# One core: the causal convolution of 64 heads, rewritten from full Toeplitz blocks to chunks of 256 samples with carried modal states

## The reference, cut to what matters

```
# layer 0: per head h a causal convolution along the 1024 samples
dt = exp(log_dt[h]);  A = -exp(log_A_real) + i*A_imag          # 64 modes per head
K[h, l] = 2*Re( sum_n C[h,n]*(exp(dt*A[h,n])-1)/A[h,n] * exp(dt*A[h,n]*l) )
u = x * (sample < length[sequence])
y = causal_conv(u, K[h]) + D[h]*u
x = x + mask * y
# layer 1: per row (1024 samples as features)
base   = x @ W.T ;  logits = x @ Wr.T + 5*onehot(language)     # 8 experts
gates  = softmax over the top 2 logits
x = x + base + 2 * sum_e gates[e] * (x @ A[e].T) @ B[e].T      # rank 16
```

## Time and profile before

| what | value |
|---|---|
| median of the runs | 749.24 us |
| profiled execution: span | 747.6 us |
| profiled execution: own time | only its span is on record; the runs lie 1.6 us above it |
| TensorE busy | 724.0 us (97%), 4453 matmuls |
| weight loads | 707.0 us (95%) |
| VectorE busy | 357.8 us (48%) |
| ScalarE busy | 282.1 us (38%) |
| GpSimd busy | 31.0 us (4%) |
| mean granted TensorE clock | 0.994 of 2.4 GHz |

### The profile page before, as it was taken

One profiled execution on the slowest core, in us unless ns is written; L12 is line 12 of the kernel. 1 busy time (PEld: TensorE's weight loads), 2 busy tenths in 40 slices (PEclk: granted clock), 3 DMA queues, 4 the chain that ended last, 5 costly groups with the idle time before them and its releaser, 6 DMA issues.

```text
span 747.6 us, 11954 instructions
## 1 busy us (share of the span) xinstructions
PE 724.0 (97%) x4453; PEld 707.0 (95%) x4453; DVE 357.8 (48%) x891; ACT 282.1 (38%) x388; POOL 31.0 (4%) x37
## 2 busy tenths in 40 slices
PE   3799999999999999999999999999999999999997
PEld 2689999999999999999999999999999999999997
DVE  8884453543454444455344444455345544334431
ACT  4755333453324433343333442345332433333111
POOL 4030100010000100001000010001000000000000
PEclk9899999999999999999999999999999999999999
DMA  7661523217221263213432152321722125321002
GB/s 241 197 192 29 130 98 113 84 28 226 55 77 67 58 196 112 84 28 97 130 112 84 28 156 83 99 84 28 226 87 60 50 68 187 112 84 29 11 20 56
DMA packets 23545, 72.99 MB, mean 98 GB/s; under 512 B 4522, under 2 KB 5866, under 8 KB 23530
## 3 DMA queue, kind: packets, MB, share of 16 engines
q1 hardware_dynamic: 18250, 56.01, 25.8%
q10 hardware_dynamic: 5280, 16.78, 6.8%
HBM read 55.71 MB, written 17.07 MB: 97 GB/s over the span
## 4 chain that ended last, share of the span: by engine, by line
PE 95%; DVE 3%; issue 1%; ACT 0%; DMA 0%; ACTq 0%; SPq 0%; DVEq 0%
PE pmg L929 55%; PE pc L889 25%; PE pmg L904 6%; PE px L895 4%; PE px L861 4%; PE pmg L850 1%; PE pmg L926 0%; DVE w_lo L648 0%; DVE ex_q L572 0%; DVE toe L627 0%; DMA logs<-in_L_cond_log_A_real 0%; ACT result L464 0%; DVE xt L704 0%; DVE toe L575 0%; DVE toe L620 0%
## 5 line engine op out<-in xcount | busy, mean ns | idle before, releaser
L929 PE MATMUL pmg<-w_hi,y_hi 128*128 128x388 f32 (+1 forms) x768 | 264.5, 344 | 0.0
L929 PE MATMUL pmg<-w_hi,y_lo 128*128 128x388 f32 (+1 forms) x768 | 260.2, 339 | 0.0
L929 PE MATMUL pmg<-w_lo,y_hi 128*128 128x388 f32 (+1 forms) x768 | 259.8, 338 | 0.0
L889 PE MATMUL pc<-u,t_hi 128*128 128x512 f32 (+4 forms) x640 | 167.5, 345 | 1.2 <-DVE t_lo L777 1.2
L929 PEld LDWEIGHTS pmg<-w_hi,y_hi 128*128 128x128 f32 x768 | 144.2, 188 | 2.0
L929 PEld LDWEIGHTS pmg<-w_hi,y_lo 128*128 128x128 f32 x768 | 144.5, 188 | 0.0
L929 PEld LDWEIGHTS pmg<-w_lo,y_hi 128*128 128x128 f32 x768 | 144.2, 188 | 0.0
L889 PE MATMUL pc<-u,t_lo 128*128 128x512 f32 (+7 forms) x512 | 124.2, 304 | 0.0
L889 PEld LDWEIGHTS pc<-u,t_hi 128*128 128x128 f32 x640 | 112.3, 188 | 8.5 <-issue 1.4
L678 DVE TENSOR_TENSOR u<-xt,u 128x1024 fp32r<-128x1024 f32 x30 | 36.8, 1226 | 118.1 <-ACT xt L422 76.6
L889 PEld LDWEIGHTS pc<-u,t_lo 128*128 128x128 f32 x512 | 82.6, 189 | 3.7
(11 more groups left out here) (160 smaller groups left out, 615.3 us busy)
## 6 DMA issues: line engine op xcount, KB each, us to landing
toe<-kpad SPq DMA_DIRECT2D x31, 1024.0 KB, 7.0
rows<-in_x SPq DMA_DIRECT2D x64, 256.0 KB, 7.3
out<-result ACTq DMA_DIRECT2D x62, 256.0 KB, 5.7
result<-in_L_cond_W SPq DMA_DIRECT2D x3, 512.0 KB, 7.7
rows<-in_L_cond_W SPq DMA_DIRECT2D x2, 512.0 KB, 6.8
toe<-in_L_cond_W SPq DMA_DIRECT2D x2, 512.0 KB, 4.6
toe<-in_L_cond_B SPq DMA_DIRECT2D x1, 512.0 KB, 5.2
xt<-in_L_cond_W SPq DMA_DIRECT2D x1, 512.0 KB, 8.5
```

Source lines behind the costliest of these rows:

```text
L889: ins = nc.tensor.matmul(pc[:, h, d:CH, :], t[s][:, h, d * P:(d + 1) * P], v[s][:, 0:n, tok], start=(d == 0 and v is u_hi and t is t_hi), ...
L929: ins = nc.tensor.matmul(pm[:, n, 0:c1 - c0], y[s][:, c, :], w[:, c, c0:c1], start=(c == 0 and y is y_hi and w is w_hi), stop=(c == CH - 1 ...
```

## The change

K is no longer made for 1024 lags but for 256 (SPAN). Inside a chunk of 256 samples the convolution is a Toeplitz product with two block lags (the diagonal one over all 8 blocks, 512 columns, and the next over every second block, 256 columns). What reaches over a chunk's edge goes through 64 complex modes per head, held as 128 real numbers: `control` multiplies the samples of chunks 0 to 2 with the powers of the modes (c_hi, c_lo, the turned table Z), `carry` rotates by a per-head factor and scans the three chunk states, and in `convolve` the states (s_hi, s_lo) are multiplied with the powers zo_hi, zo_lo and added to chunks 1 to 3. All products take three passes.

New for each pair are `turn_powers` (4 transposes of Z into the upper half of px), `split_ctr`, `split_obs`, `copy_states` (4 ScalarE instructions), `carry` (18 VectorE instructions in five stages, each behind a wait on the one before) and `split_states`. Gone are `copy_far`, two additions in `merge`, and three quarters of the Toeplitz tile. K and the powers are made for 4 heads (DUO), once in two pairs, and the table Z is 4 x 256 = 1024 wide; its argument and magnitude are made by 8 ScalarE instructions with per-partition scales instead of two GpSimd products. GpSimd stages per-head scalars. The loop body is two pairs. toe, t_hi, t_lo and the c tiles have one buffer, so the load of the next four heads' Toeplitz tile waits for t_lo of the last pair that used the old one. The start is reordered, with 73 parameter steps.

```diff
-            def convolve(b, m, first=False, turned=True):
...
-                    for d in range(CH):
-                        n = CH - d
-                        near = d < FAR
-                        for t, v in ((t_hi, u_hi), (t_hi, u_lo), (t_lo, u_hi)) if near else ((t_lo, u_hi),):
-                            ins = nc.tensor.matmul(pc[:, h, d:CH, :], t[s][:, h, d * P:(d + 1) * P], v[s][:, 0:n, tok],
-                                                   start=(d == 0 and v is u_hi and t is t_hi), stop=d == CH - 1)
+            def convolve(b, m, first=False):
...
+                for h in range(2):
+                    tok = slice(h * SEQS, (h + 1) * SEQS)
+                    three(pc[:, h, :, :], (t_hi[:, h, 0:P], t_lo[:, h, 0:P]),
+                          (u_hi[s][:, :, tok], u_lo[s][:, :, tok]), True, False)
+                    three(pc[:, h, 1:CH:2, :], (t_hi[:, h, P:SPAN], t_lo[:, h, P:SPAN]),
+                          (u_hi[s][:, 0:CH:2, tok], u_lo[s][:, 0:CH:2, tok]), False, False)
+                pe.wait_ge(zhi_ready, i + 1)
+                pe.wait_ge(zlo_ready, i + 1)
+                pe.wait_ge(shi_ready, i + 1)
+                pe.wait_ge(slo_ready, i + 1)
+                for h in range(2):
+                    for q in range(2):
+                        at = slice(q * P, (q + 1) * P)
+                        ins = three(pc[:, h, 2 + q:CH:2, :], (zo_hi[s][:, h, at], zo_lo[s][:, h, at]),
+                                    (s_hi[:, h, :, :], s_lo[:, h, :, :]), False, q == 1)
+                ins.then_inc(conv_done, 1)
+            def control(b, m):
...
+                for h in range(2):
+                    tok = slice(h * SEQS, (h + 1) * SEQS)
+                    for q in range(2):
+                        ins = three(v_psum[:, h, :, :], (c_hi[:, h, q, :], c_lo[:, h, q, :]),
+                                    (u_hi[s][:, q:CH - 2:2, tok], u_lo[s][:, q:CH - 2:2, tok]), q == 0, q == 1)
 # TensorE, one step
                 if rows_left:
                     turn_rows(b, m + 2)
-                convolve(b, m + 1, turned=rows_left)
-                if kernels and m == 1:
-                    make_kernels(b + 1)
-                project(b, m)
+                convolve(b, m + 1)
+                pe.wait_ge(yhi_ready, 2 * b + m + 1)
+                pe.wait_ge(ylo_ready, 2 * b + m + 1)
+                project_bank(b, m, 0)
+                if rows_left:
+                    control(b, m + 2)
+                if ahead:
+                    turn_powers(b, m + 3)
+                if kernels and m == 1:
+                    make_kernels(b + 2)
+                project_bank(b, m, 1)
+                project_bank(b, m, 2, kernels)
 # ScalarE, one step
+                if kernels and m == 1:
+                    waves(b + 2)
+                if rows_left:
+                    split_toe(b, m + 2)
+                split_y(b, m + 1)
+                if ahead:
+                    split_obs(b, m + 3)
+                ratios(b, m)
+                if rows_left:
+                    copy_states(b, m + 2)
+                if ahead:
+                    split_ctr(b, m + 3)
+                if kernels and m == 0:
+                    act.wait_ge(gen_staged, b + 1)
+                    turns_of(None, True)
+                    magnitudes(None, True)
+                if kernels and m == 1:
+                    copy_kernels(b + 2)
+                split_gated(b, m)
+                if rows_left:
+                    split_states(b, m + 2)
+                finish(b, m)
 # VectorE, one step
                 if rows_left:
                     split_rows(b, m + 2)
                 merge(b, m + 1)
+                if rows_left:
+                    split_toe(b, m + 2)
+                if kernels and m == 1:
+                    powers(b + 2)
+                split_y(b, m + 1)
+                if ahead:
+                    split_obs(b, m + 3)
+                route(b, m)
+                if ahead:
+                    split_ctr(b, m + 3)
+                if rows_left:
+                    dve.wait_ge(scan_staged, b + m // 2 + 1)
+                    carry(b, m + 2)
+                split_gated(b, m)
+                if kernels and m == 0:
+                    angles(b + 2)
+                if rows_left:
+                    split_states(b, m + 2)
+                if kernels and m == 1:
+                    first_samples(b + 2, bass.ds((b + 2) * DUO, DUO))
 # VectorE, carry: 18 instructions, five stages
+                for h in range(2):
+                    add(S[:, h, :, :], swapped[:, h, :, :], k(C2_IM, h), S[:, h, :, :])
+                for h in range(2):
+                    ins = vec.tensor_scalar(R[:, h, :, :], swapped[:, h, two, :], k(C2_RE, h), None, ALU.mult)
+                ins.then_inc(scan, 1)
+                dve.wait_ge(scan, SCAN * i + 1)
+                for h in range(2):
+                    add(R[:, h, :, :], v_psum[:, h, two, :], k(C2_NIM, h), R[:, h, :, :])
+                for h in range(2):
+                    ins = add(S[:, h, 1, :], S[:, h, 0, :], k(A_RE, h), S[:, h, 1, :])
+                ins.then_inc(scan, 1)
...
 # SyncE
+            def load_toe(g, split=None):
+                sp.wait_ge(k_stored, 16 * g + 16)
+                if split is not None:
+                    sp.wait_ge(tlo_ready, split)
...
+                if ahead:
+                    sp.wait_ge(px_full, i + 2)
+                    load_rows(b, m + 3)
+                if kernels and m == 1:
+                    store_kernels(b + 2)
+                    load_toe(b + 2, 2 * b + 4)
```

More of the change, by code:

```diff
@@ L76, in cond_resid_kernel @@
         xt = [sb(f"xt{s}", [P, CH, P]) for s in range(2)]
[L77 to L82, removed]
+        u_hi = [sb(f"u_hi{s}", [P, CH, P], F32R) for s in range(2)]
+        u_lo = [sb(f"u_lo{s}", [P, CH, P], F32R) for s in range(2)]
+        t_hi = sb("t_hi", [P, 2, SPAN], F32R)
+        t_lo = sb("t_lo", [P, 2, SPAN], F32R)
+        c_hi = sb("c_hi", [P, 2, 2, P], F32R)
+        c_lo = sb("c_lo", [P, 2, 2, P], F32R)
+        zo_hi = [sb(f"zo_hi{s}", [P, 2, SPAN], F32R) for s in range(2)]
+        zo_lo = [sb(f"zo_lo{s}", [P, 2, SPAN], F32R) for s in range(2)]
+        state = sb("state", [P, 2, CARRIED, SEQS])
+        swapped = sb("swapped", [P, 2, CARRIED, SEQS])
+        turned_s = sb("turned_s", [P, 2, CARRIED - 1, SEQS])
+        s_hi = sb("s_hi", [P, 2, CARRIED, SEQS], F32R)
+        s_lo = sb("s_lo", [P, 2, CARRIED, SEQS], F32R)
         y_hi = [sb(f"y_hi{s}", [P, CH, P], F32R) for s in range(2)]
@@ L372, in _ @@
[L372 to L386 removed]
+            at = pos_far[:, :].unsqueeze(1).to_broadcast([P, HEADS, FARS])
@@ L522, in _ @@
+                finish(b, m)
+            with act.Fori(0, LOOPS) as b:
+                for m in range(2):
+                    step(b, m)
+            step(LOOPS, 0, kernels=False)
+            step(LOOPS, 1, ahead=False, kernels=False)
+            step(LOOPS + 1, 0, rows_left=False, ahead=False, kernels=False)
+            ratios(LOOPS + 1, 1)
+            split_gated(LOOPS + 1, 1)
+            finish(LOOPS + 1, 1, last=True)
             act.wait_ge(result_dma[0], START + 16 * PAIRS)
@@ L862, in turn_rows, with three @@
                 ins.then_inc(px_full, 1)
-            def convolve(b, m, first=False, turned=True):
-                i, s = BODY * b + m, m % 2
+            def three(out, left, right, first, last):
+                (l_hi, l_lo), (r_hi, r_lo) = left, right
+                for n, (l, r) in enumerate(((l_hi, r_hi), (l_hi, r_lo), (l_lo, r_hi))):
+                    ins = nc.tensor.matmul(out, l, r, start=first and n == 0, stop=last and n == 2,
+                                           skip_group_check=True)
+                return ins
@@ L953, in _ @@
-            convolve(0, 0, first=True)
-            for k in range(LATE, WTILES):
-                turn_weight(k)
-            def step(b, m, rows_left=True, kernels=True):
+            turn_weight(0)
+            turn_weight(1)
+            pe.wait_ge(par_dve, C1_STEPS)
+            turn_parameters(C1_RE)
+            pe.wait_ge(par_dve, C2_STEPS)
+            turn_parameters(C2_RE)
+            pe.wait_ge(uhi_ready, 1)
+            turn_powers(0, 0)
+            turn_weight(2)
+            turn_weight(3)
@@ new lines, in _ @@
+            pe.wait_ge(gk_ready, 1)
+            pe.wait_ge(prm_ready, 4)
+            make_kernels(0, staged=False)
+            control(0, 0)
+            turn_powers(0, 1)
+            for k in range(4, 7):
+                turn_weight(k)
+            turn_rows(0, 1)
+            turn_weight(7)
+            turn_weight(8)
+            convolve(0, 0, first=True)
+            control(0, 1)
+            turn_powers(0, 2)
+            pe.wait_ge(k_copied, 1)
+            make_kernels(1, staged=False)
@@ new lines, in step @@
+                project_bank(b, m, 1)
+                project_bank(b, m, 2, kernels)
+            with pe.Fori(0, LOOPS) as b:
+                for m in range(2):
```

(8 more changed lines are left out.)

890 lines of the change are left out of this document (494 added, 396 removed).

## The result

The changed kernel takes 754.65 us (754.19 to 755.12, four runs) against 749.23 (749.13 to 749.26): ratio 1.0073, interval 1.0059 to 1.0087. It is slower by 0.7% where 2.6% faster was forecast. The span is 753.0 us, forecast 728.4. Ratios compare runs at the usual clock alone: one execution of a later kernel (e6) took 991.73 us at a granted clock of 0.66, where its others had 0.97 to 0.98, nothing here explains it, and it is left out of that kernel's figures.

What follows compares the result with a forecast made beforehand. TensorE was taken as the bound, VectorE's queue to gt_lo stalling each step 0.45 us. Start 71.3, even steps 306.8, odd 294.0, then 19.6, 17.7 and 19.0: span 728.4, forecast 730 us against 749.24, range 710 to 756.

Steps and rivals of the forecast that it cites:

- loop starts: Start of the loop: forecast at 67.3 us against 45.39 before, plus 2 us low clock at the first convolution.
- steps 29, 30 and the rest: End of the kernel: 19.6 us without kernels and powers, 17.7 without rows and control, last projection to span end 19.0.
- The step that failed: VectorE's queue in a step: u_lo starts 4.19 us in, or 4.63 where the loop's edge falls, in each even step.
- The table load's price: ScalarE: a table load takes 1.28 us with no drain behind it; the skill page says 2.66 in all.
- The queue's other terms: VectorE and ScalarE ahead of gt_lo: carry 4.6 us (ends 3.3 and 5.8), four state copies 1.6, overlay 1.35.
- slower queue: Rival: VectorE's queue sets the step, with carry at 5.8 us between c_lo and gt_lo; 767 us, chance 15%.
- point of decision: The extra VectorE time per step from which the change turns out slower: 0.57 us (17.7 / 31), carry at 5.2.
- late reload: Rival: the Toeplitz load takes 7.0 us, t_hi ends at 8.6, even steps move by 1.35; 750 us, chance 12%.
- TensorE's own time: A step on TensorE alone: 20.0 us, 20.55 in odd steps with kernel matmuls; 58 us saved in all.
- The Toeplitz reload: Load of 512 KB taken as 5.5 us, landing 6.5 us into the even step; t_hi ends at 7.1, just hidden.
- The start: Before the loop: first convolution at 49.8 us; with 4 us for the low clock, the start costs 26 us more.

Runs made afterwards that it cites:

- e6: Changed kernel with one dummy exponential ahead of the loop, plus 15 one-column VectorE copies between carry and gt_lo: 765.16 us, ratio 1.0206 to the kernel before.
- first experiment: Changed kernel plus one dummy exponential after the start's last sine, so no table load stands at the loop's head: 736.98 us, ratio 0.9842 to the kernel before.

## Why the prediction was wrong, step by step

The spans are compared, forecast 728.4 against 753.0:

| term | forecast | measured | difference |
|---|---|---|---|
| loop starts (67.3 and 2 for the first convolution) | 69.3 | 76.13 | +6.8 |
| step 0 (even, low clock) | 22.45 | 22.78 | +0.3 |
| even steps 2 to 26 | 13 x 20.45 | 13 x 21.74 | +16.7 |
| step 28 | 20.45 | 20.31 | -0.1 |
| odd steps | 14 x 21.0 | 14 x 21.04 | +0.6 |
| steps 29, 30 and the rest | 56.3 | 56.6 | +0.3 |

**The step that failed** is the first of VectorE's queue in even steps: "u_lo starts 4.19 us in, or 4.63 where the loop's edge falls". Measured 5.75 (376.69 to 382.44); in the odd step 4.14 (forecast 4.19). Without the load it is 4.47 (first experiment), and gt_lo then starts 18.00 us into the step, where 18.2 was forecast: the rest of the queue was added up right. The difference is the load at the loop's head. The prediction counted the loads that a step's own functions ask for, sine and ratio, and left out the one that the loop's two entries ask for. The row for a load's price was there; the count was wrong. As the queue was late already (by 0.15 us, forecast 0.45), all of the load came out at the end: 1.29 us in each of 13 even steps, 16.8 us (17.7 between the medians), more than the 5.4 between the kernels. The second term that failed is the start, 6.8 us too short.

**The table load's price** was right: 1.28 us, and xt starts 0.01 behind it (379.10, 380.39). The Trainium skill ("ScalarE: Activation LUTs", What ACT_TABLE_LOAD costs) has 2.66 with the drain; by that figure 13 loads would have given an estimated 35 us back where 16.8 came. The trace disagrees with the drain here too.

**The queue's other terms** were near: `carry` 4.42 (forecast 4.6, ends 3.3 and 5.8), state copies 1.7 (1.6), overlay 1.34 (1.35). The rival "slower queue" was right in its place, VectorE's queue up to gt_lo, but it blamed `carry`. Its point of decision, 0.57 us more per step, is 17.7 / 31; against 749.24 it should be 19.2 / 31 = 0.62. Its share and the others' of "slower" add up to 24%, not 20%. That 754.65 lies under the range's upper end of 756 is luck: that end was made of a late reload and a `carry` of 5.4, and neither came.

**TensorE's own time** was too low, and the stalls hid it. Forecast 20.0 and 20.55, measured 20.29 and 21.03 where it waits for nothing. The odd step came out at 21.0 without any stall: a right total of two wrong terms. The 12 matmuls of 192 columns in `control`, in the even step above:

```profile
385.21 0.25 PE L1038 MATMUL px<-u_hi,c_hi 128*128 128x192 f32 x1
...
386.52 0.60 PE L1086 MATMUL px<-ident,Z 128*128 128x128 f32 x4
```

They take 1.31 us, 0.11 each from start to start, forecast 0.095 and 1.15; the convolution takes 3.49 (377.48 to 380.97), forecast 3.4. That is 0.25 of the 0.29 that even steps are longer. The four kernel matmuls add 0.74 to an odd step (21.03 - 20.29), forecast 0.55. The weights change from one matmul to the next in these passes. The Trainium skill ("TensorE: Matmul & The Clock Gate", Back-to-back issue gap) gives N/2.4 + 2.5 ns for a matmul without its weight load, 0.083 us for 192 columns and 0.216 for 512, and says that a stream of weight loads and matmuls is spaced otherwise, 0.081 us at 128 columns and 0.131 at 512. The traces show 0.11 at 192 and 0.23 at 512; they contradict the 0.131. Per step TensorE saves 22.1 - 20.66 = 1.4 us, 46 over the 32 pairs where I had 58.

**The Toeplitz reload** is hidden, as forecast, with more to spare than forecast: 4.7 us from issue to landing (forecast 5.5). The step shown is one of two in which t_hi waits for it at all (0.25), and y_hi then waits 1.80 for the overlay.

**The start.** I had both last tiles turned early, at the end of the first convolution's stretch; the second waits for the banks of the first (4.1 us by the run with the other banks). The first convolution begins at 51.40 (forecast 49.8). The low clock costs 2.8 us there instead of 2, and 2.3 in the first step instead of 2. A loop start of 65 to 73 us was named as a sign of being right; it was 76.13.

**Balance.** TensorE alone would give back 46 us. The start takes 30.7 of them (45.4 to 76.1), the even steps 2 to 26 take 18.7 (1.44 each above TensorE's own 20.29), the low clock of the first step 2.3. That is some 5.5 more than there was; the spans differ by 5.4. Without the load the time is 736.98 against 730 forecast, and the later start is about the rest.

## What to carry to other kernels

Count the table loads of a loop from both of its entries: where the code ahead of it leaves another table than its body, a load stands at the head in each turn, and one cheap function with the right table ahead of the loop takes it away. When work is added to an engine, add up its queue from the first instruction of the step to the one that the bounding engine waits for; put the awaited one ahead of what can wait (in stage gaps of `carry` here) rather than make the engine faster. A longer start costs its length, and the low clock behind its idle stretches of TensorE besides: here the choice of a bank was worth 4.1 us once and filled idle stretches 5.6.

## What the runs showed that I had not expected

- An instruction that needs no table (a copy) carries a 1.28 us table load, 14 times, because of where it stands in the loop.
- 115 to 145 transposes in the start that nobody reads make the kernel faster: TensorE turned the first rows in 1.09 us instead of 1.97, and the first step took 20.3 to 20.5 us instead of 22.8.
- One more 512 KB transfer ahead on the same queue makes a load of the same size land 7.4 us after its issue instead of 4.7.
- 15 one-column copies on VectorE take 0.99 us, and ahead of gt_lo they cost 28.2 us in 29 steps, behind it nothing.
- TensorE's granted clock can fall inside the loop: with the late reload it did in four of the even steps, to 0.95 to 0.97 over the step.
